# A graph network's sparse products: a fifth ring slot for the last set, and each window's first adjacency made ahead, across the window's border

## The reference, cut to what matters

```python
# layer 2 (self loops are added apart; dinv = 1/sqrt(degree))
h = x @ W
agg = segment_sum(h[src] * dinv[src] * dinv[dst], dst, n) + b
# layer 3
msg = edge_weight[:, None] * x[src]
out = x + segment_sum(msg, dst, n)
h = relu(out @ W1 + b1); y = h @ W2 + b2
```

## Time and profile before

| | us |
|---|---|
| median of three runs | 10348.83 |
| the profiled execution's own time | 10350.83 |
| its span | 10349.3 |
| PE busy | 8097.8 (78%) |
| DVE busy | 8014.5 (77%) |
| ACT busy | 4511.3 (44%) |
| POOL busy | 1392.5 (13%) |
| stage g, from and to | 8346 to 8943 |
| stage x, from and to | 9093 to 10222 |

### The profile page before, as it was taken

How to read it: one execution, slowest core, us unless ns; L and a number is a source line. 1 busy time by engine, 2 the same in 40 slices (tenths; PEclk the granted TensorE clock), 3 DMA queues, 4 the chain that set the end, 5 groups by cost and what they waited for, 6 DMA issues and landing times. The chain is left out here.

```text
span 10349.3 us, 308524 instructions
## 1 busy us (share of the span) xinstructions
PE 8097.8 (78%) x93825; PEld 6641.3 (64%) x93826; DVE 8014.5 (77%) x16711; ACT 4511.3 (44%) x9126; POOL 1392.5 (13%) x1711
## 2 busy tenths in 40 slices
PE   2335668858887557999967997998999779579996
PEld 0232226747776447999965665447999756378886
DVE  4997778979998666666668997777888777878887
ACT  0220002246664115666644443886777556333333
POOL 0110002200000004666630000000000012100000
PEclk7555555579998558999988998999999889799998
DMA  2000004524443112333326886884555300000000
GB/s 56 0 4 11 5 5 152 181 93 161 162 161 124 37 37 102 124 122 122 125 71 213 274 271 215 291 291 139 144 143 145 102 6 6 3 4 3 3 3 14
DMA packets 613604, 1067.61 MB, mean 103 GB/s; under 512 B 121042, under 2 KB 266713, under 8 KB 607126
## 3 DMA queue, kind: packets, MB, share of 16 engines
q1 hardware_dynamic: 489510, 892.28, 27.2%
q10 hardware_dynamic: 113040, 161.93, 4.2%
q0 software_dynamic: 10976, 12.53, 0.4%
HBM read 870.64 MB, written 195.84 MB: 103 GB/s over the span
## 5 line engine op out<-in xcount | busy, mean ns | idle before, releaser
L2583 POOL TENSOR_TENSOR acc<-acc,m_sum 128x544 f32<-128x544 f32 (+1 forms) x637 | 810.7, 1273 | 1222.1 <-ACT m_sum L2550 1181.8
L2447 DVE TENSOR_TENSOR m_msg<-m_vps,m_msg 128x512 f32<-128x512 f32 (+1 forms) x637 | 427.5, 671 | 416.4 <-PE m_vps L2488 378.6
L2512 PE MATMUL m_sps<-m_msg,m_oh 128*128 128x136 f32 x4900 | 697.5, 286 | 0.0
L2919 PE MATMUL u_sps<-u_r,u_oh 128*128 128x129 f32 x4900 | 657.3, 276 | 29.0 <-ACT u_r L2875 29.0
L1545 ACT COPY sp_adj_x<-sp_aps_x 128x512 f32<-128x512 f32 (+1 forms) x637 | 362.4, 569 | 722.1 <-PE sp_aps_x L1516 722.1
L1532 PE MATMUL sp_out_x<-x,sp_adj_x 128*128 128x128 f32 x4802 | 671.5, 284 | 0.0
L2152 PE MATMUL s_qps<-q_parts,s_oht 128*128 128x128 bf16 x7203 | 511.8, 220 | 198.0 <-DVE s_oht L1599 146.0
L1516 PE MATMUL sp_aps_x<-sp_ohw_x,sp_oh_x 128*128 128x128 bf16 x7350 | 536.3, 221 | 166.5 <-DVE sp_ohw_x L1483 166.4
L2903 PE MATMUL u_zps<-fcs,u_a 128*128 128x128 f32 x4916 | 654.7, 276 | 7.3 <-ACT u_a L2868 7.3
L2919 PEld LDWEIGHTS u_sps<-u_r,u_oh 128*128 128x128 f32 x4900 | 598.4, 192 | 38.1 <-issue 38.1
L2512 PEld LDWEIGHTS m_sps<-m_msg,m_oh 128*128 128x128 f32 x4900 | 610.1, 191 | 0.0
(11 more groups left out here) (590 smaller groups left out, 19807.1 us busy)
## 6 DMA issues: line engine op xcount, KB each, us to landing
u_e<-e_tiles SPq DMA_DIRECT2D x591, 256.0 KB, 2.8
e_tiles<-t_es ACTq DMA_DIRECT2D x588, 256.0 KB, 4.2
g_e<-e_tiles SPq DMA_DIRECT2D x588, 256.0 KB, 4.5
s_rows<-bucket_rows SPq DMA_DIRECT2D x148, 768.0 KB, 4.1
m_rows<-bucket_rows SPq DMA_DIRECT2D x148, 768.0 KB, 4.1
bs_krow<-bucket_keys SPq DMA_DIRECT2D x50, 1600.0 KB, 6.9
t_rows<-bucket_rows SPq DMA_DIRECT2D x148, 384.0 KB, 5.2
s_rows<-bucket_rows SPq DMA_DIRECT2D x49, 896.0 KB, 5.0
```

The costliest lines, as they stand in the source:

```text
L2447: nc.vector.tensor_tensor(m4[:, :, 0:D].rearrange("p j (h d) -> p j h d", h=H), vps[x][:, 0:n * D].rearrange("p (j h d) -> p j h d", j=n, ...
L2512: last = nc.tensor.matmul(sps[x][:, at:at + M], oh[x][:, j * P:(j + 1) * P], msg[x][:, j * M:(j + 1) * M], start=True, stop=True)
L2583: nc.gpsimd.tensor_tensor(at, at, sums[x][:, 0:n * M], ALU.add).then_inc(added, 1)
L2919: last = nc.tensor.matmul(sps[:, :], oh[x][:, j * P:(j + 1) * P], zr[x][:, j * D1:(j + 1) * D1], start=(q == 0 and j == 0), stop=(q == las ...
```

## The change

`Ring(NQ, 4, True)` gives set 12 a fifth slot: sets 0 to 11 use slots 0 to 3 three times a window, set 12 uses slot 4 once. On DVE, TensorE and ACT the first set's step is taken out of the loop for window 0, and each window ends by doing the next window's: DVE pairs it before it weighs set 12, TensorE makes it between product(11) and product(12) and then makes set 1 ahead of product(0), ACT copies it before the total. After the last window one such set is made that nobody uses; SP loads one more list for it (row 0) and DVE weighs it after its loop.

```diff
-def load_lists(nc, B, sp, lst, nw, lists_free, lists_go, lists_in, lists_ready):
-
-    with sp.Fori(0, nw) as w:
+def load_lists(nc, B, sp, lst, nw, lists_free, lists_go, lists_in, lists_ready, one_more=False):
+
+    def load(w, row):
         sp.wait_ge(lists_free, w + 1)
         ...
+    with sp.Fori(0, nw) as w:
+        load(w, w)
+    if one_more:
+        load(nw, 0)
...
-    R = Ring(NQ, 4)
+    R = Ring(NQ, 4, True)
...
+                def pair(w, q):
+                    r, at = R.slot(q), (w & 1) * B.cols
+                    if q == 0:
+                        dve.wait_ge(lists_ready, w + 1)
+                    dve.wait_ge(adj_made[r], R.before(w, q) + 1)
+                    ...
+                pair(0, 0)
                 with dve.Fori(0, nw) as w:
-                    at = (w & 1) * B.cols
-                    dve.wait_ge(lists_ready, w + 1)
...
-                    pair(0)
                     for q in range(NQ):
-                        if q + 1 < NQ:
-                            pair(q + 1)
+                        pair(*((w, q + 1) if q + 1 < NQ else (w + 1, 0)))
                         if weighted:
-                            weigh(q)
+                            weigh(w, q)
 
                     dve.wait_ge(oh_made[R.slot(last_q)], R.before(w, last_q) + 1)
                     dve.sem_inc(lists_free, 1)
+                if weighted:
+                    weigh(nw, 0)
...
+                make(0, 0)
                 with pe.Fori(0, nw) as w:
-                    for q in range(NQ + 1):
-                        if q < NQ:
...
-                        if q >= 1:
-                            p = q - 1
...
+                    for q in range(NQ):
+                        make(*((w, q + 1) if q + 1 < NQ else (w + 1, 0)))
+                        r = R.slot(q)
+                        pe.wait_ge(adj_copied[r], R.before(w, q) + 2)
+                        if q == 0:
+                            pe.wait_ge(gathered, w + 1)
+                        if q == last_q:
+                            pe.wait_ge(over_set, w + 1)
+                        for t in range(B.held(q)):
+                            ...
+                        last.then_inc(used[r], 1)
...
+                keep(0, 0)
                 with act.Fori(0, nw) as w:
-                    for q in range(NQ):
-                        ...
+                    for q in range(1, NQ):
+                        keep(w, q)
+                    keep(w + 1, 0)
                     r = R.slot(last_q)
                     act.wait_ge(used[r], R.before(w, last_q) + 2)
                     act.wait_ge(total_free, w + 1)
                     nc.scalar.copy(total[:, :], out[:, :]).then_inc(gathered, 1)
...
-                    pool.wait_ge(used[r], R.before(w, 0) + 1)
+                    pool.wait_ge(used[r], R.done(w, r) + 1)
```

More of the change, by code:

```diff
@@ L1416, in user_before @@
         return (0, same[at - 1]) if at else (-1, same[-1])
-def load_lists(nc, B, sp, lst, nw, lists_free, lists_go, lists_in, lists_ready):
-    with sp.Fori(0, nw) as w:
+def load_lists(nc, B, sp, lst, nw, lists_free, lists_go, lists_in, lists_ready, one_more=False):
+    def load(w, row):
         sp.wait_ge(lists_free, w + 1)
         sp.sem_inc(lists_go, 1)
-        sp.dma_start(lst[:, bass.ds((w & 1) * B.cols, B.cols)], B.lists[bass.ds(w * P, P), :]).then_inc(lists_in, 16)
+        sp.dma_start(lst[:, bass.ds((w & 1) * B.cols, B.cols)], B.lists[bass.ds(row * P, P), :]).then_inc(lists_in, 16)
         sp.wait_ge(lists_in, w * 16 + 16)
         sp.sem_inc(lists_ready, 1)
+    with sp.Fori(0, nw) as w:
+        load(w, w)
+    if one_more:
+        load(nw, 0)
 def pair_one_hot(nc, k, out, lst, at, pairs):
@@ L1462, in _ @@
             def _(sp):
-                load_lists(nc, B, sp, lst, B.windows(sp, s), lists_free, lists_go, lists_in, lists_ready)
+                load_lists(nc, B, sp, lst, B.windows(sp, s), lists_free, lists_go, lists_in, lists_ready, True)
             @block.vector
@@ L1469, in _ @@
                 dve.sem_inc(lists_free, 2)
-                with dve.Fori(0, nw) as w:
-                    at = (w & 1) * B.cols
-                    dve.wait_ge(lists_ready, w + 1)
[L1474 to L1487, removed]
-                    pair(0)
+                def pair(w, q):
[3 more added lines that the diff above has]
+                    dve.wait_ge(adj_made[r], R.before(w, q) + 1)
+                    pair_one_hot(nc, k, oh[r], lst, at + q * FG, B.held(q) // 2).then_inc(paired[r] if weighted else oh_made[r], 1)
@@ new lines, in weigh @@
+                def weigh(w, q):
+                    r, n, at = R.slot(q), B.held(q) // 2, (w & 1) * B.cols
+                    dve.wait_ge(paired[r], R.before(w, q) + 1)
+                    return nc.vector.tensor_tensor(
+                        ohw[r][:, 0:n * 6 * P].rearrange("p (x v t) -> p x v t", v=P, t=2),
+                        oh[r][:, G * P:(G + 2 * n) * P].rearrange("p (q y) -> p q y", q=n).unsqueeze(2).broadcast_to([P, n, 3, 2 * P]),
+                        lst[:, bass.ds(at + q * FG + 8, 6 * n)].rearrange("p (x t) -> p x t", t=2).unsqueeze(2).broadcast_to([P, 3 * n, P, 2]),
+                        ALU.mult).then_inc(oh_made[r], 1)
@@ L1503, in _ @@
                     pe.sem_inc(used[r], 1)
-                with pe.Fori(0, nw) as w:
-                    for q in range(NQ + 1):
-                        if q < NQ:
[L1507 to L1519, removed]
-                        if q >= 1:
-                            p = q - 1
[L1522 to L1533, removed]
@@ new lines, in make @@
+                def make(w, q):
+                    r = R.slot(q)
+                    pe.wait_ge(oh_made[r], R.before(w, q) + 1)
+                    pe.wait_ge(adj_copied[r], R.before(w, q) + 1)
+                    for t in range(B.held(q)):
+                        part = aps[r][:, t * P:(t + 1) * P]
+                        at_src = of_pair(oh[r][:, :], P, t)
+                        if weighted:
+                            w5 = ohw[r][:, :].rearrange("p (q c v t) -> p q c v t", q=2, c=3, t=2)
+                            for c in range(3):
+                                last = nc.tensor.matmul(part, at_src, w5[:, t // 2, c, :, t % 2], start=(c == 0), stop=(c == 2))
+                        else:
+                            last = nc.tensor.matmul(part, at_src, of_pair(oh[r][:, :], P, G + t), start=True, stop=True)
+                    last.then_inc(adj_made[r], 1)
@@ new lines, in _ @@
+                make(0, 0)
+                with pe.Fori(0, nw) as w:
+                    for q in range(NQ):
+                        make(*((w, q + 1) if q + 1 < NQ else (w + 1, 0)))
+                        r = R.slot(q)
+                        pe.wait_ge(adj_copied[r], R.before(w, q) + 2)
[3 more added lines that the diff above has]
+                            pe.wait_ge(over_set, w + 1)
+                        for t in range(B.held(q)):
+                            tile = q * G + t
+                            rhs = table[:, tile * width:(tile + 1) * width] if tile < s.NB else \
+                                over[:, (tile - s.NB) * width:(tile - s.NB + 1) * width]
+                            last = nc.tensor.matmul(out[:, :], adj[r][:, t * P:(t + 1) * P], rhs, start=(tile == 0), stop=(tile == AT - 1))
+                        last.then_inc(used[r], 1)
@@ L1539, in _, with keep @@
                     act.sem_inc(adj_copied[r], 1)
-                with act.Fori(0, nw) as w:
-                    for q in range(NQ):
[L1542 to L1545, removed]
+                def keep(w, q):
+                    r = R.slot(q)
+                    act.wait_ge(adj_made[r], R.before(w, q) + 2)
+                    act.wait_ge(used[r], R.before(w, q) + 1)
+                    nc.scalar.copy(adj[r][:, 0:B.held(q) * P], aps[r][:, 0:B.held(q) * P]).then_inc(adj_copied[r], 1)
+                keep(0, 0)
+                with act.Fori(0, nw) as w:
+                    for q in range(1, NQ):
+                        keep(w, q)
+                    keep(w + 1, 0)
                     r = R.slot(last_q)
```

## The result

| | before | after |
|---|---|---|
| median of four runs, us | 10350.71 | 10217.76 |
| the profiled execution's own time | 10350.83 | 10220.17 |
| its span | 10349.3 | 10218.6 |

The ratio of the times is 0.9868, 95% interval 0.9855 to 0.9881. Predicted were 10215 us with a range of 10204 to 10240.

A forecast was written before the change was run, and what follows sets the result against it. TensorE (PE) was taken to bound both stages. Gains of 122.2 and 13.9 less costs of 1.0 and 0.6 make 134.5 us, from 10350.83 to 10216.3; with the median 2.0 lower 10214.3, stated as 10215, range 10204 to 10240.

The forecast's parts named there:

- Stage x, 122.2 us: In the f32 weighted stage, the window period falls to 20.44 us over 48 windows, gaining 122.2 us.
- Stage g, 13.9 us: In the bf16 unweighted stage, the window period falls to 11.81 us with a new 0.75 us stall, gaining 13.9 us.
- DVE at nothing: DVE in stage x has 1.4 us of slack a window and runs sets ahead, so it costs nothing.
- Past the end: The unused set's make and ACT copy before the last total cost 0.7 us in x, 0.3 in g.
- Semaphores: Five more semaphores in each stage, cleared by GpSimd at its end, cost 0.3 us each stage, 0.6 in all.
- Loop border and lists at nothing: TensorE's loop border, with work queued on both sides, and the next window's list loads, released a period earlier, cost nothing.
- Rival A: In stage x the clock dips stay, costing 15.6 us: time 10231 us, chance 0.12.
- B: At the borders ACT's late total copy takes g's gain and costs in x too: 10239 us, chance 0.14.
- D: In stage x the denser stream drops the clock to 1.2 GHz: 10419 us at 10 half-clock windows, chance 0.02.
- E: TensorE's issue slows as its pauses go, so both window periods stay 22.66 and 12.10 us: 10351 us, chance 0.03.
- C: Everything meets: no stall in x, ACT overlaps in g, no clearing cost: 10211 us, chance 0.07.
- The 81 ns: Skill page's gap per weight load and matmul: a 23.9 us window in x, so no gain there; the prediction rejected it.

The follow-up runs named there:

- the early make: Changed kernel, next window's first make moved ahead of product(11): 0.9851; also with two output banks in g, 0.9841, and there with DVE copying the total, 0.9840.
- the total first: Changed kernel, but ACT copies the total before the next window's first adjacency: ratio 0.9902, 100 us under the kernel before.
- two banks: Changed kernel with two output banks alternating by window in both stages: ratio 0.9869, 138 us under the kernel before.

## Why the prediction was right, point by point

- *Stage x, 122.2 us.* Measured 1103.3 - 981.1 = 122.2. The total's copy came at 2.74 (2.70 to 2.77 predicted), the period was 20.44 as written. The last 0.03 us of it agree by luck: the prediction added them as a stall behind the total's copy, and there is none. TensorE itself was sized that much too short. The first two instructions of a product behind a make take 0.28 us to issue (9577.76 to 9578.04), the next two 0.22 (to 9578.26), so each change from make to product costs some 0.05 us. The sum counts it 12.5 times a window, the program has it 13 times (+0.03), and with the early make 12 times, which fits the 20.39 of those three kernels. The slot is 108 us of the change; making ahead takes the rest, by putting ACT's copy of the first adjacency beside product(12) and make(1').
- *Stage g, 13.9 us.* Measured 580.8 - 568.0 = 12.8. The first product came 2.38 us after the last make (2.36 to 2.45 predicted), TensorE's new stall was 0.73 us by issue (0.75). The step before it was off: the cast started 0.50 us after its make (8659.85 to 8660.35), not 0.43, and the latency behind the total's copy was 0.06, not 0.13; the two errors cancel. That what is late next is the bank with ACT's cast ahead of it was argued from rows then; the total first (+0.32 us), the early make (-0.32) and two banks (-0.11) show it.
- *DVE at nothing.* Right for the time, but the slack was mis-sized: 1.4 us were read from DVE's busy time, 0.84 was there (a mean; 1.07 in the short windows, 0.6 in the long). Busy time leaves out what an engine must wait for by its own order.
- *Past the end, 0.7 and 0.3 us.* From the clearing of acc to the first total: g 8345.06 to 8365.00 = 19.94 us (8341.53 to 8361.09 = 19.56 before), +0.38 where 0.3 was expected; x 9077.54 to 9108.40 = 30.86 (9086.42 to 9117.10 = 30.68), +0.18 where 0.7 was expected.
- *Semaphores, 0.3 us each.* From the start of the last total's copy to the next stage's first vector operation 3.73 us before and 10093.57 - 10089.52 = 4.05 after x; 5.53 and 5.86 after g. So 0.32 and 0.33.
- *Loop border and lists at nothing.* In x product(12) and make(1') follow one another at 9577.76 and 9578.26, across the border; no wait for lists is named. The evidence was read wrong, though: the 62 rows are matmul instructions, two for each f32 product (1274 in 49 windows of 13), so they pass two borders, not four. And the border is not free everywhere: in g with the early make it costs 0.06 us, and no run shows what decides that.
- *Rival A* fell: not one long window. In the kernel with making ahead alone 7 of 48 were 24.2 us long again, with a gap of 1.73 us before the first make; the granted clock is 0.50 from 9172 to 9174 in one of them. Three more vector operations leave gaps of 0.2 to 0.6 us before makes, and the clock stays at 1.00. Which gap lets it fall was not settled: most windows with the long gap kept it. The falls are not strewn at random either: the seven come at every seventh window, the ten before the change at every fourth but for one.
- *Rivals B to E.* B, D and E fell: the total's copy was not late (2.74 us in x), the clock was 1.00 in stage x and the stream closed up (20.44). C had it right that the stall in x is 0 and that ACT overlaps in g (cast and total start 0.49 us apart), but the clearing was not free and its time, 10211, was not reached.
- *The 81 ns* of the Trainium skill (TensorE: Matmul & The Clock Gate, "Back-to-back issue gap", for a weight load and matmul of 128 columns in a sustained stream) did not show: a make of 12 still takes 0.69 us (9577.07 to 9577.76) with no wait of TensorE named from the first total of the stage to the last, and the window 20.44 us, not 23.9.
- *What stays open.* All work ahead of stage g took 3.5 us more in the profiled execution after than before (clearing of acc at 8345.06, against 8341.53), with the same instructions. Runs of one kernel differ by as much (10211.89 to 10220.17), so I give it no cause. It is most of the 3.9 us between the sum for the profiled execution (10216.3) and its time (10220.17); g's missing 1.1 us is the next.

## What to carry to other kernels

When a ring of n slots has one set left over, look at who refills the shared slot: the engine that runs ahead may be stopped just where the others need its lead. A step made ahead helps only if its inputs are there; put ahead of work that is ready, it blocks that work. Before the edit, write the border down as start times on each engine with the latencies of the rows: that gave both periods within 0.02 us here, though in x by luck in the last 0.03. An engine's slack is not its busy time taken from the period: its waits for its own work come off it as well.

## What the runs showed of the hardware that was not expected

A matmul whose output address depends on a register cost TensorE about 0.20 us once a window in g, where the address is worked out between the wait and the first matmul (0.34 us from cast to product in place of 0.13; 0.20 us behind a make of four matmuls, with no wait at all and with the offset put into a register at the head of the loop). In x, behind a make of 12 matmuls, it cost 0.05. ACT starts an operation 0.37 us after the start of a 0.48 us copy, so two copies in a row cost less than their sum. GpSimd's add of 128x128 elements took from 0.5 to 17.8 us in stage x with three more vector operations there (0.9 in the changed kernel), and the long ones ended where DVE first paused; why it goes the one way or the other, no run shows.
